# Front attention: two heads gathered in one round, two more copies on VectorE, three engines in a new order

## The reference, cut to what matters

```python
q, k, v = heads(x @ Wq), heads(x @ Wk), heads(x @ Wv)       # each (4, 16, 1024, 8)
scores = einsum('bhid,bhjd->bhij', q, k)
rel = einsum('bhid,pd->bhip', q, rel_key)                   # 256 relative positions
bias = take_along_axis(rel, clip(j - i + 255, 0, 255), 3)   # skewed: one row shift per query
logits = where(j <= i, (scores + bias) * scale, -inf)
out = softmax(logits) @ v                                   # then @ Wo, residual, and six layers
```

## Time and profile before

| | |
|---|---|
| median of 3 runs | 4100.39 us (4099.25 to 4101.06) |
| the profiled execution | 4098.77 us, span 4096.9 us, mean granted clock 0.977 |
| front attention, first `rel` 0 to last division | 82 to 927 us of the span |
| busy over the span | PE 3940.0, ACT 3771.9, DVE 3450.4, POOL 2329.4, PEld 2914.0 us |

### The profile page before, as it was taken

One profiled execution on the slowest core, in us unless ns is written; L12 is line 12 of the kernel. 1 busy time (PEld: TensorE's weight loads), 2 busy tenths in 40 slices (PEclk: granted clock), 3 DMA queues, 4 the chain that ended last, 5 costly groups with the idle time before them and its releaser, 6 DMA issues. The chain is left out here.

```text
span 4096.9 us, 125398 instructions
## 1 busy us (share of the span) xinstructions
PE 3940.0 (96%) x43636; PEld 2914.0 (71%) x43636; DVE 3450.4 (84%) x8234; ACT 3771.9 (92%) x7378; POOL 2329.4 (57%) x2684
## 2 busy tenths in 40 slices
PE   4999999997999999999999999999999999999995
PEld 2566666663777777777777777777777777777774
DVE  4788888875988888888888888888888888888884
ACT  4899999985999999999999999999999999999995
POOL 4000000006777777777777777777777777777773
PEclk7899999997999999999999999999999999999997
DMA  6777777752111111111111111111111111111111
GB/s 180 223 232 231 228 228 230 234 176 75 49 44 47 46 40 44 44 49 46 39 44 49 44 49 35 49 44 49 44 38 46 49 44 44 49 36 48 44 49 54
DMA packets 249745, 347.67 MB, mean 85 GB/s; under 512 B 45104, under 2 KB 206364, under 8 KB 249116
## 3 DMA queue, kind: packets, MB, share of 16 engines
q1 hardware_dynamic: 249244, 340.94, 27.9%
HBM read 151.06 MB, written 82.85 MB: 57 GB/s over the span
## 5 line engine op out<-in xcount | busy, mean ns | idle before, releaser
L1468 PE MATMUL la_ps<-la_Wqkv,la_xsT 128*128 128x512 f32 x2304 | 1172.8, 602 | 6.8 <-DVE X L1164 6.8
L1164 DVE TENSOR_TENSOR X<-la_ps,la_tab 128x1024 f32<-128x1024 f32 x768 | 938.2, 1222 | 102.0 <-ACT la_sq L1312 95.6
L1094 POOL TENSOR_TENSOR la_rt<-X 128x512 f32<-128x512 f32 x384 | 495.9, 1291 | 589.9 <-PE la_ps L1483 436.6
L1111 POOL TENSOR_TENSOR la_rt<-la_rt,la_rn 128x1024 f32<-128x1024 f32 x384 | 722.4, 1902 | 27.5
L1173 DVE TENSOR_REDUCE la_ssum<-la_sq 128x8 f32<-128x512 f32 x768 | 511.1, 666 | 0.0
L1312 ACT ACTIVATE la_sq<-la_ps 128x512 f32<-128x512 f32 x768 | 464.9, 605 | 34.8 <-PE la_ps L1468 30.1
L1095 POOL TENSOR_TENSOR la_rt<-X 128x512 f32<-128x512 f32 x384 | 495.6, 1291 | 0.0
L527 POOL COPY at_vh<-V 128x64 f32 (+1 forms) x64 | 15.1, 236 | 783.9 <-PE at_ps L726 782.7
L1499 PEld LDWEIGHTS la_ps<-la_kT,la_qB 128*64 128x64 f32 x12288 | 390.4, 138 | 85.1 <-issue 73.7
L1468 PEld LDWEIGHTS la_ps<-la_Wqkv,la_xsT 128*128 128x128 f32 x2304 | 362.3, 190 | 120.3 <-issue 75.3
L1499 PE MATMUL la_ps<-la_kT,la_qB 128*64 128x64 f32 x12288 | 432.9, 224 | 0.0
(11 more groups left out here) (204 smaller groups left out, 9046.2 us busy)
## 6 DMA issues: line engine op xcount, KB each, us to landing
at_band<-skew_scratch SPq DMA_DIRECT2D x64, 1536.0 KB, 7.3
la_vs<-la_v SPq DMA_DIRECT2D x192, 384.0 KB, 3.5
skew_scratch<-at_R SPq DMA_DIRECT2D x64, 1024.0 KB, 6.7
la_vs<-la_v SPq DMA_DIRECT2D x192, 128.0 KB, 3.4
la_Wqkv<-in_wqkv SPq DMA_DIRECT2D x28, 384.0 KB, 5.4
at_qh<-qt_scratch SPq DMA_DIRECT2D x64, 144.0 KB
at_kh<-kt_scratch SPq DMA_DIRECT2D x64, 144.0 KB
la_W<-in_L_ffn_W SPq DMA_DIRECT2D x24, 341.0 KB, 5.2
```

The source lines that it names most:

```text
L1094: e.tensor_tensor(dst[:, :, 0, :], c[:, :, 0, :], s[:, :, 1, :], ALU.add)
L1111: e.tensor_tensor(heads(rt, w), heads(rt, w), wide(rn[:, w * H:(w + 1) * H], D), ALU.mult)\
L1164: e.tensor_tensor(dst.rearrange("p f (h d) -> p f h d", d=D), ps[:, c % 2, :].rearrange("p (h d) -> p h d", d=D).unsqueeze(1).to_broadcast ...
L1468: e.matmul(ps[:, c % 2, :], xsT[:, m * P:(m + 1) * P], Wqkv[:, ds(layer(n) % 2, 1), c * 512:(c + 1) * 512], start=True, stop=True)\
```

## The change

VectorE copies blocks 2 and 8 as well. The values of an even head keep columns 0 to 8 and those of an odd head columns 9 to 17 of a 32-wide tile (`vh`); `drain` copies an even head's bank O into `part` and adds an odd head's to it, and `gather` and `over_sum` run only at odd heads, over 18 columns a tile. The bodies of DVE, ACT and PE are laid out anew with lags of up to 5, and `rounds` unrolls eight turns ahead of its loop where it unrolled four. SP's body and its order are as they were.

```diff
-BY_DVE = (3, 6, 10)
-DEEPEST_A = 4
+BY_DVE = (2, 3, 6, 8, 10)
+DEEPEST_A = 5
...
-    for g in range(ring):
-        body(Turn(g, g, count, ring))
-    with e.Fori(1, count // ring) as turn:
+    for g in range(2 * ring):
+        body(Turn(g, g % ring, count, ring))
+    with e.Fori(2, count // ring) as turn:
...
             def drain(n, m, u):
                 e.wait_ge(pv_mm.sem, pv_mm.v(n, 2 * u + 1))
-                e.wait_ge(g_mm.sem, before(g_mm, n, u, 1, JJ))
-                e.tensor_copy(part[:], ps[:, O_BANK, :]).then_inc(o_ev.sem, 1)
+                if m % 2:
+                    e.wait_ge(o_ev.sem, o_ev.v(n - 1, u + 1))
+                    e.tensor_tensor(part[:, u, :], ps[:, O_BANK, :], part[:, u, :], ALU.add).then_inc(o_ev.sem, 1)
+                else:
+                    e.wait_ge(g_mm.sem, g_mm.v(n // 2 - 1, u + 1))
+                    e.tensor_copy(part[:, u, :], ps[:, O_BANK, :]).then_inc(o_ev.sem, 1)
...
             def over_sum(n, m, u):
+                if m % 2 == 0:
+                    return
...
             def body(t):
-                for n, m in t.back(4):
-                    copied(n, m, 6)
+                for n, m in t.back(0):
+                    least(n, m, 0)
...
                 if g == 0:
                     e.wait_ge(vh_ev.sem, vh_ev.v(n))
-                if g < 2:
-                    e.wait_ge(on.sem, before(on, n, u, 1, JJ))
+                if g == 0:
+                    e.wait_ge(o_ev.sem, o_ev.v(n - 1))
+                elif g == 1 and m % 2:
+                    e.wait_ge(on.sem, on.v(n // 2, 1))
+                elif g == 1:
+                    e.wait_ge(o_ev.sem, o_ev.v(n, 1))
+                    e.wait_ge(on.sem, on.v(n // 2 - 1))
...
             def gather(n, m, u):
+                if m % 2 == 0:
+                    return
                 e.wait_ge(o_ev.sem, o_ev.v(n, u + 1))
+                if u == 1 and not (isinstance(n, int) and n == HEADS_A - 1):
+                    e.wait_ge(o_ev.sem, o_ev.v(n + 1, 1))
```

More of the change, by code:

```diff
@@ L403, in first_attention @@
     JJ = TB // G
+    VW = D_A + 1
     NJ = sum(G * (u + 1) for u in range(JJ))
@@ L413, in first_attention @@
         pT = t.sb("pT", [P, 2, G, G * P])
-        part, sel = t.sb("part", [P, G * P]), t.sb("sel", [P, D_A + 1])
-        rc, cell = t.sb("rc", [P, G]), t.sb("cell", [P, TB])
+        part, sel = t.sb("part", [P, JJ, G * P]), t.sb("sel", [P, 2 * VW])
+        rc, cell = t.sb("rc", [P, G, 2]), t.sb("cell", [P, TB])
         ps = t.psum()
@@ L428, in first_attention @@
         pv_mm = t.mark("pv", GROUPS, RING_A)
-        o_ev, g_mm, on = t.mark("oe", JJ), t.mark("gm", JJ, 1), t.mark("on", JJ, 1)
+        o_ev, g_mm, on = t.mark("oe", JJ, 1), t.mark("gm", JJ, 1), t.mark("on", JJ, 1)
         c_far = t.mark("cf", TB - BAND // P)
@@ L521, in _ @@
             e.wait_ge(s_set, 1)
-            e.memset(vh[:, :, :, D_A:D_A + 1], 1.0).then_inc(s_set, 1)
-            e.wait_ge(s_set, 2)
+            for m in range(RING_A):
+                one = m % 2 * VW + D_A
+                e.memset(vh[:, m, :, one:one + 1], 1.0).then_inc(s_set, 1)
+            e.wait_ge(s_set, 1 + RING_A)
             def head_of_v(n, m):
                 e.wait_ge(pv_mm.sem, pv_mm.v(n - RING_A))
-                e.tensor_copy(vh[:, m, :, 0:D_A], V[:, ds(n // H_A * TB, TB), ds(n % H_A * D_A, D_A)])\
+                at = m % 2 * VW
+                e.tensor_copy(vh[:, m, :, at:at + D_A], V[:, ds(n // H_A * TB, TB), ds(n % H_A * D_A, D_A)])\
                     .then_inc(vh_ev.sem, 1)
@@ L536, in _ @@
         def _(e):
-            for mark in (mn_ev, tD, on):
+            for mark in (mn_ev, tD, on, o_ev):
                 mark.open(e)
@@ L567, in drain @@
                 e.wait_ge(pv_mm.sem, pv_mm.v(n, 2 * u + 1))
-                e.wait_ge(g_mm.sem, before(g_mm, n, u, 1, JJ))
-                e.tensor_copy(part[:], ps[:, O_BANK, :]).then_inc(o_ev.sem, 1)
-            def over_sum(n, m, u):
[L572 to L577, removed]
+                if m % 2:
[4 more added lines that the diff above has]
+                    e.tensor_copy(part[:, u, :], ps[:, O_BANK, :]).then_inc(o_ev.sem, 1)
@@ new lines, in over_sum @@
+            def over_sum(n, m, u):
+                if m % 2 == 0:
+                    return
+                o = ps[:, O_BANK, 0:G * 2 * VW].rearrange("p (i r d) -> p i r d", i=G, r=2)
+                e.wait_ge(g_mm.sem, g_mm.v(n // 2, u + 1))
+                e.reciprocal(rc[:].unsqueeze(3), o[:, :, :, D_A:VW]).then_inc(c_on.sem, 1)
+                e.wait_ge(c_on.sem, c_on.v(n // 2, u + 1))
+                tile, col = n // H_A * TB + G * u, n % H_A * D_A - D_A
+                e.tensor_tensor(O[:, ds(tile, G), ds(col, 2 * D_A)].rearrange("p i (r d) -> p i r d", r=2),
+                                o[:, :, :, 0:D_A], rc[:].unsqueeze(3).to_broadcast([P, G, 2, D_A]), ALU.mult)\
@@ L578, in over_sum @@
                     .then_inc(on.sem, 1)
             def body(t):
-                for n, m in t.back(4):
-                    copied(n, m, 6)
-                    over_sum(n, m, 0)
-                for n, m in t.back(3):
+                for n, m in t.back(0):
+                    least(n, m, 0)
+                for n, m in t.back(2):
+                    copied(n, m, 10)
+                for n, m in t.back(0):
+                    least(n, m, 1)
+                    far_least(n, m, 3)
+                    least(n, m, 2)
+                    least(n, m, 3)
+                    far_least(n, m, 4)
@@ L587, in body @@
                     least(n, m, 5)
[L588 to L600, removed]
+                for n, m in t.back(1):
+                    copied(n, m, 2)
                     copied(n, m, 3)
                 for n, m in t.back(2):
[L603 to L607, removed]
+                    drain(n, m, 1)
+                for n, m in t.back(0):
+                    far_least(n, m, 6)
+                    far_least(n, m, 7)
+                    least(n, m, 6)
+                for n, m in t.back(1):
+                    copied(n, m, 6)
                     drain(n, m, 0)
+                for n, m in t.back(0):
+                    least(n, m, 7)
+                for n, m in t.back(1):
+                    copied(n, m, 8)
                 for n, m in t.back(2):
-                    far_least(n, m, 4)
-                    least(n, m, 3)
+                    over_sum(n, m, 1)
+                for n, m in t.back(1):
+                    over_sum(n, m, 0)
             rounds(e, body, HEADS_A, RING_A, DEEPEST_A)
@@ L641, in body @@
                 for n, m in t.back(3):
+                    exp(n, m, 2)
                     exp(n, m, 3)
+                for n, m in t.back(1):
+                    rel(n, m, 3)
                 for n, m in t.back(4):
-                    copied(n, m, 8)
-                    copied(n, m, 9)
+                    copied(n, m, 0)
+                    copied(n, m, 1)
                 for n, m in t.back(3):
                     exp(n, m, 4)
-                for n, m in t.back(4):
-                    copied(n, m, 11)
-                for n, m in t.back(3):
                     exp(n, m, 5)
@@ L653, in body @@
                     rel(n, m, 0)
[L654 to L657, removed]
+                for n, m in t.back(4):
+                    copied(n, m, 4)
+                    copied(n, m, 5)
                 for n, m in t.back(0):
@@ L660, in body @@
                 for n, m in t.back(3):
-                    copied(n, m, 2)
+                    exp(n, m, 6)
+                for n, m in t.back(4):
+                    copied(n, m, 7)
+                for n, m in t.back(3):
                     exp(n, m, 7)
+                for n, m in t.back(4):
+                    copied(n, m, 9)
                 for n, m in t.back(2):
                     exp(n, m, 0)
-                    exp(n, m, 1)
                 for n, m in t.back(0):
                     rel(n, m, 2)
-                for n, m in t.back(3):
-                    copied(n, m, 4)
-                    copied(n, m, 5)
                 for n, m in t.back(2):
[L672 to L676, removed]
+                    exp(n, m, 1)
+                for n, m in t.back(4):
+                    copied(n, m, 11)
             rounds(e, body, HEADS_A, RING_A, DEEPEST_A)
@@ L731, in gather @@
             def gather(n, m, u):
+                if m % 2 == 0:
+                    return
                 e.wait_ge(o_ev.sem, o_ev.v(n, u + 1))
+                if u == 1 and not (isinstance(n, int) and n == HEADS_A - 1):
+                    e.wait_ge(o_ev.sem, o_ev.v(n + 1, 1))
                 for i in range(G):
                     k = WIN * min(G, G * u + i + 1)
-                    mm = e.matmul(ps[:, O_BANK, i * (D_A + 1):(i + 1) * (D_A + 1)],
-                                  part[0:k, i * P:(i + 1) * P], sel[0:k, :], start=True, stop=True)
+                    mm = e.matmul(ps[:, O_BANK, i * 2 * VW:(i + 1) * 2 * VW],
```

(47 more changed lines are left out.)

## The result

| | before | after |
|---|---|---|
| device time, median of 4 runs (lowest to highest) | 4100.73 us (4099.25 to 4101.26) | 4334.32 us (4322.03 to 4340.66) |
| profiled execution, its span | 4098.77, 4096.9 us | 4330.46, 4328.7 us |
| granted TensorE clock, mean over the span | 0.977 | 0.940 |

The changed kernel takes 1.0567 times as long, 95% interval 1.0541 to 1.0592: 234 us more. 4190 with a range of 4140 to 4225 had been forecast. The direction was right; the time lies 109 us above the range.

The account below looks back on a forecast made before the run. A DMA ring and PE's list bound the kernel within tenths; the ring would lengthen to 5.72 + 8.4 = 14.1 us. 59 x (14.1 - 12.65) = 86, + 4, on 4098.8, + 1.6 gave 4190 us, range 4140 to 4225.

Parts of the forecast that it names:

- the ring: Turn to turn: `rel` 0, `scores` 7, `least` 7, band DMA, keys' loads, next `rel` 0; 14.1 us, chance 0.73.
- PE's wait: PE idle before each `rel` 0 for the keys' DMA, about 2 us a turn, taken to be hidden and free.
- block 3 held: DVE's in-order list waits for block 3's transpose behind `rel` 0: 5.72 us to the band's issue; otherwise 5.4.
- The other half: From the band's issue on SP to the next `rel` 0, sizes and order unchanged: 8.4 us, between 8.10 and 9.40.
- The work that goes: Fewer gathers, reciprocals and multiplications, two copies from ACT to DVE: busy PE 11.4, DVE 10.9, ACT 10.4 us, end unmoved.
- the ring's own half: From `rel` 0 to the band's issue on SP, through PE and DVE: 4.08 us before, 5.72 forecast.
- signs of being wrong: `rel` 0 without a gap, band issued under 5 us behind `rel` 0, or the stretch's granted clock under 1.00.
- the clock falls: PE's clock drops in its new waits before `rel` 0: 59 turns at 2.8 us more, 4270 us, chance 0.04.
- The ends: Turns ahead of head 4 cost 0; the deeper lag in the last turns adds 4 us, between 0 and 8.

## Why the prediction was right about the ring and wrong about PE's wait

- *The ring* was right: the steps and their order are those forecast, and block 3 held. At full clock `rel` 0 to the band takes 5.34 us where 5.72 was forecast. The two `far_least` take 1.33 from start to start where I summed 1.61: in the rows that I took, each was followed by the `least` that needs its result, and here it isn't. Block 3's copy takes 0.21 instead of 0.35; the rest agrees within 0.06. The other half is 8.48 (8.4). The turn is 13.8 for 14.1; at that, with the forecast's 4 us at the end, the sum gives 4098.8 + 59 x 1.15 + 4 + 1.6 = 4172, and with the clock held 4172 to 4178 was measured.
- *The work that goes* was right: a full-clock turn holds 11.44 us of PE, 10.67 of DVE and 10.77 of ACT (forecast 11.4, 10.9, 10.4), and none of it shortened the turn.
- *The step that failed* is "the ring hides it, and PE will sit before `rel` 0 for some 2 us". PE did sit there, 1.3 to 3.1 us. I took that idle time as free. It cost the clock, and half clock in the first 7 us of a turn falls on the ring's own half, where PE feeds DVE: 8.5 instead of 5.34. That is 162 of the 234 us, shown by the kernels that fill the wait. Of the prediction's signs of being wrong, the one that came true is the granted clock under 1.00.
- *The rival "the clock falls"* had the right cause, a chance of 0.04 and too low a time (4270). I priced it by one turn at the start (15.45) instead of putting half clock into the ring, which would have doubled PE's steps there. And I weighed it down by one stretch of the tail with 77% busy at 1.00, against two at the start where PE had waited and the clock was low. The Trainium skill ("TensorE: Matmul & The Clock Gate", section "HAM oscillation — how this bites in real kernels") tells of a kernel whose clock falls anew in every tile because PE waits for that tile's load. The trace agrees: 44 of 59 turns begin at the lower level, behind waits for the keys of 1.4 to 3.1 us.
- *The ends* cost 8.5 us behind head 63 instead of 4; part of that stretch runs at a lower clock (0.95 from 1100 to 1150). In the kernel with 16 matmuls it is 5.4.
- What decides whether the clock falls stays open. Full-clock turns stand behind waits of 1.45 and 1.65 us, half-clock ones behind 1.41 and 1.68; four short matmuls kept it, in 54 of 59 turns, with waits up to 2.2; and one addition lost it in 14 of 59 turns with waits of at most 0.8.

## What to carry to other kernels

Where the last DMA of a turn waits for compute and the next turn's first load is queued behind it, that is a ring: sum it before anything else, and try first to issue the load ahead. If a change makes PE wait once a turn, price the turn at both clocks; the half-clock price goes into every PE step on the ring, not into PE's busy time. Work taken from a busy engine shows only once the ring is shorter than that engine's list.

## What the runs showed of the hardware that was not expected

- With one wait of about 2 us a turn in an otherwise busy PE (87% over 730 us), the granted clock was 0.83, with 0.53 in the first 6.9 us of a long turn.
- With four matmuls of 0.11 us each at the head of that wait it was 0.99.
- Shorter waits are not always safer: 0.97 was granted with waits of at most 0.8 us for DVE's copy, 0.99 with waits up to 1.3 at the same place.
